# Cross-attention of a decoder layer: half blocks in one order, two projections and two output rows in a run, six places for rotated queries

## The reference

```python
q = (query @ Wq).reshape(nb, q_len, 32, 128).transpose(0, 2, 1, 3)
k = (key @ Wk).reshape(nb, q_len, 8, 128).transpose(0, 2, 1, 3)
v = (value @ Wv).reshape(nb, q_len, 8, 128).transpose(0, 2, 1, 3)
q = q * cos + _rotate_half(q) * sin
k = k * cos + _rotate_half(k) * sin
k, v = jnp.repeat(k, 4, axis=1), jnp.repeat(v, 4, axis=1)
scores = jnp.einsum('bhqd,bhkd->bhqk', q, k) / jnp.sqrt(jnp.float32(128))
scores = jnp.where(mask == 0, jnp.float32(-1000000000.0), scores)
attn = jax.nn.softmax(scores, axis=-1)
x = jnp.einsum('bhqk,bhkd->bhqd', attn, v)
return x.transpose(0, 2, 1, 3).reshape(nb, q_len, 32 * 128) @ Wo
```

## Time and profile before

| | busy us in the span | share |
|---|---|---|
| TensorE matmuls (PE) | 1502.7 | 93% |
| TensorE weight loads (PEld) | 1192.1 | 74% |
| VectorE (DVE) | 1132.3 | 70% |
| ScalarE (ACT) | 458.3 | 29% |
| GpSimd (POOL) | 481.1 | 30% |

### The profile page before, as it was taken

How to read it: one execution, slowest core, us unless ns; L and a number is a source line. 1 busy time by engine, 2 the same in 40 slices (tenths; PEclk the granted TensorE clock), 3 DMA queues, 4 the chain that set the end, 5 groups by cost and what they waited for, 6 DMA issues and landing times. The chain is left out here.

```text
span 1607.8 us, 25367 instructions
## 1 busy us (share of the span) xinstructions
PE 1502.7 (93%) x9824; PEld 1192.1 (74%) x9824; DVE 1132.3 (70%) x1819; ACT 458.3 (29%) x802; POOL 481.1 (30%) x411
## 2 busy tenths in 40 slices
PE   7899978999999569999999999999999999998698
PEld 5688856677777357787778878877877787786476
DVE  3555333688888677787887787787887877886454
ACT  4111133565555221222221221222222212211311
POOL 4322212222222123332432423433333324231022
PEclk9999989999999779999999999999999999999799
DMA  7455211000000221001020110020020201000211
GB/s 231 134 180 171 100 51 39 1 14 21 8 2 1 87 72 52 27 21 60 27 66 14 40 53 27 28 66 22 19 66 27 61 19 40 14 27 1 89 46 59
DMA packets 79107, 83.89 MB, mean 52 GB/s; under 512 B 9824, under 2 KB 50928, under 8 KB 78736
## 3 DMA queue, kind: packets, MB, share of 16 engines
q1 hardware_dynamic: 68976, 63.42, 12.4%
q10 hardware_dynamic: 9216, 16.78, 3.2%
q0 software_dynamic: 800, 2.11, 0.4%
HBM read 59.22 MB, written 23.07 MB: 51 GB/s over the span
## 5 line engine op out<-in xcount | busy, mean ns | idle before, releaser
L1211 POOL TENSOR_TENSOR p_q_rot<-p_ra,p_rb 128x512 f32<-128x512 f32 x128 | 166.9, 1304 | 286.7 <-DVE p_rb L565 286.7
L981 PE MATMUL p_ps_y<-p_wo_hi,p_o_hi 128*128 128x512 f32 x512 | 212.8, 416 | 5.6 <-DVE p_o_lo L1130 5.4
L75 PE MATMUL p_ps_q<-b_xt_hi,p_wq_hi 128*128 128x512 f32 x512 | 211.3, 413 | 0.0
L982 PE MATMUL p_ps_y<-p_wo_lo,p_o_hi 128*128 128x512 f32 x512 | 203.2, 397 | 0.0
L983 PE MATMUL p_ps_y<-p_wo_hi,p_o_lo 128*128 128x512 f32 x512 | 203.0, 396 | 0.0
L76 PE MATMUL p_ps_q<-b_xt_lo,p_wq_hi 128*128 128x512 f32 x512 | 202.4, 395 | 0.0
L77 PE MATMUL p_ps_q<-b_xt_hi,p_wq_lo 128*128 128x512 f32 x512 | 201.2, 393 | 0.0
L1203 POOL TENSOR_TENSOR p_pn<-p_p,p_inv 128x512 f32<-128x512 f32 x64 | 66.8, 1043 | 298.2 <-DVE p_inv L1110 298.2
L1052 ACT ACTIVATE p_o_hi<-p_ps_o 128x512 fp32r<-128x512 f32 x128 | 69.5, 595 | 281.0 <-PE p_ps_o L968 281.0
L1140 DVE TENSOR_TENSOR x_sb<-p_ps_y,x_sb 128x512 f32<-128x512 f32 x128 | 88.0, 688 | 87.3 <-PE p_ps_y L983 87.3
L563 DVE TENSOR_TENSOR p_ra<-p_ps_q,b_cos_t 128x512 f32<-128x512 f32 x128 | 85.9, 671 | 59.8 <-PE p_ps_q L77 56.4
(11 more groups left out here) (179 smaller groups left out, 3163.2 us busy)
## 6 DMA issues: line engine op xcount, KB each, us to landing
p_raw_q<-in_wq SPq DMA_DIRECT2D x36, 256.0 KB, 3.2
v_scratch<-p_v_out SPq DMA_DIRECT2D x32, 256.0 KB, 2.7
k_scratch<-p_k_out SPq DMA_DIRECT2D x32, 256.0 KB, 2.1
p_k_t<-k_scratch ACTq DMA_DIRECT2D x32, 256.0 KB, 2.6
p_v_in<-v_scratch ACTq DMA_DIRECT2D x32, 256.0 KB, 2.8
p_raw_o<-in_wo SPq DMA_DIRECT2D x32, 256.0 KB, 3.6
x_sb<-in_x SPq DMA_DIRECT2D x16, 256.0 KB, 3.1
out<-p_yb SPq DMA_DIRECT2D x16, 256.0 KB, 2.0
```

Of the source, the lines that this page charges most:

```text
L75: nc.tensor.matmul(out, lh, rh, start=(c == 0), stop=False)
L981: nc.tensor.matmul(ps_y[t][:, :], oh, w_hi["o"][h][:, :], start=(h == 0), stop=False)
L982: nc.tensor.matmul(ps_y[t][:, :], oh, w_lo["o"][h][:, :], start=False, stop=False)
L1211: nc.gpsimd.tensor_tensor(q_rot[:, h, :], ra[:, :], rb[:, :], ALU.add).then_inc(q_added, 1)
```

## The change

TensorE's order becomes the same in each half `n`: M(n-1), T(n), S(n+1), two Q, O(n-1, 0), O(n-1, 1), with M(63) and its two O behind the loop. `heads_ahead(n)` names the two Q: in an even half heads 2 and 3 of the next `it`, in an odd half heads 0 and 1 of the one behind it. In front of the loop stand now Q(1,0) and Q(1,1), and only then S(0). `q_rot` has six places instead of four, used in turn (`place`), and the wait of `add_terms` follows that ring.

The raw buffers for q and o are now the same four, so that a load of o waits for the split of q in the same buffer and the other way round. The o weights are waited for head by head in `output`. The low parts of the o weights are made by VectorE for heads 0 and 1 and by GpSimd for heads 2 and 3. The splits for the next group lie in steps 1 (o), 4 and 5 (q) of a group's eight halves. For group 0, ScalarE's exponential of half 0 stands ahead of the four o splits; VectorE does `rotate(1, 0)`, `rotate(1, 1)`, `shift(0)`, two o splits and `invert(0)`; GpSimd does two adds, two o splits and `normalise_p(0)`. The orders of ScalarE, VectorE and GpSimd in the loop follow TensorE's. The buffers keep their total size, and number and sizes of all DMAs and operations are the same.

```diff
-        raw = {"q": [m.sb(f"raw_q{i}", [P, HIDDEN]) for i in range(2)], "o": [m.sb(f"raw_o{i}", [P, HIDDEN]) for i in range(H)]}
+        RING = H + 2
+        raw = [m.sb(f"raw{h}", [P, HIDDEN]) for h in range(H)]
...
-        q_rot = m.sb("q_rot", [P, H, BLOCK])
+        q_rot = m.sb("q_rot", [P, RING, BLOCK])
...
             def load_q(g, h):
-                need(sp, ready["q"], 4 * g + h - 1)
-                sp.dma_start(raw["q"][h % 2][:, :].rearrange("p (c d) -> p c d", c=KC),
-                             wq_dram[:, :, (g * H + h) * D2:(g * H + h + 1) * D2]).then_inc(raw_in["q"][h % 2], 16)
+                need(sp, o_ready[h], g)
+                sp.dma_start(raw[h][:, :].rearrange("p (c d) -> p c d", c=KC),
+                             wq_dram[:, :, (g * H + h) * D2:(g * H + h + 1) * D2]).then_inc(raw_in[h], 16)
 
             def load_o(g, h):
-                need(sp, ready["o"], 4 * (g - 1) + h + 1)
-                sp.dma_start(raw["o"][h][:, :], wo_dram[(g * H + h) * D2:(g * H + h + 1) * D2, :]).then_inc(raw_in["o"][h], 16)
+                need(sp, q_ready, 4 * g + h + 1)
+                sp.dma_start(raw[h][:, :], wo_dram[(g * H + h) * D2:(g * H + h + 1) * D2, :]).then_inc(raw_in[h], 16)
...
-        def split_o_lo(dve, g, h):
+            nc.scalar.activation(w_hi["o"][h][:, :], raw[h][:, :], ACT.Copy).then_inc(part_hi["o"], 1)
+
+        def split_o_lo_vector(dve, g, h):
             need(dve, part_hi["o"], 4 * g + h + 1)
-            nc.vector.tensor_tensor(w_lo["o"][h][:, :], raw["o"][h][:, :], w_hi["o"][h][:, :], ALU.subtract).then_inc(ready["o"], 1)
+            nc.vector.tensor_tensor(w_lo["o"][h][:, :], raw[h][:, :], w_hi["o"][h][:, :], ALU.subtract).then_inc(o_ready[h], 1)
+
+        def split_o_lo_pool(pool, g, h):
+            need(pool, part_hi["o"], 4 * g + h + 1)
+            nc.gpsimd.tensor_tensor(w_lo["o"][h][:, :], raw[h][:, :], w_hi["o"][h][:, :], ALU.subtract).then_inc(o_ready[h], 1)
+
+        def place(it, h):
+
+            return (it * H + h) % RING
+
+        def heads_ahead(n):
+
+            return [(n // 2 + 1, 2), (n // 2 + 1, 3)] if n % 2 == 0 else [(n // 2 + 2, 0), (n // 2 + 2, 1)]
...
-                need(pe, ready["o"], 4 * (n // 2 // NB) + H)
                 need(pe, y_added, n * UT + t - 1)
                 for h in range(H):
+                    need(pe, o_ready[h], n // 2 // NB + 1)
...
+            queries(1, 0)
+            queries(1, 1)
             scores(0)
-            for it in range(ITS):
-                n = 2 * it
-                queries(it + 1, 0)
+            for n in range(HALVES):
+                if n > 0:
+                    mix(n - 1)
+                turn(n)
                 scores(n + 1)
+                for it, h in heads_ahead(n):
+                    queries(it, h)
                 output(n - 1, 0)
-                queries(it + 1, 1)
-                turn(n)
                 output(n - 1, 1)
-                queries(it + 1, 2)
-                mix(n)
-                queries(it + 1, 3)
-                output(n, 0)
-                turn(n + 1)
-                output(n, 1)
-                scores(n + 2)
-                mix(n + 1)
+            mix(HALVES - 1)
             output(HALVES - 1, 0)
...
+            exponentials(0)
             for h in range(H):
                 split_o_hi(act, 0, h)
-            for it in range(ITS):
-                n, g, b = 2 * it, it // NB, it % NB
+            for n in range(HALVES):
+                it, g, step = n // 2, n // (2 * NB), n % (2 * NB)
                 outputs_hi(n - 1)
-                exponentials(n)
-                values_hi(it)
-                if b == NB - 1 and g + 1 < KVH:
+                turned_hi(n)
+                if n % 2 == 0:
+                    values_hi(it)
+                if step == 1 and g > 0:
+                    for h in range(H):
+                        split_o_hi(act, g, h)
+                if step == 4 and g + 1 < KVH:
+                    split_q_hi(act, g + 1, 0)
+                    split_q_hi(act, g + 1, 1)
+                if step == 5 and g + 1 < KVH:
+                    split_q_hi(act, g + 1, 2)
                     split_q_hi(act, g + 1, 3)
                 exponentials(n + 1)
-                turned_hi(n)
-                load_kv(it + 1)
-                if b == 0 and g > 0:
-                    for h in range(H):
-                        split_o_hi(act, g, h)
-                outputs_hi(n)
-                if b == NB - 2 and g + 1 < KVH:
-                    split_q_hi(act, g + 1, 0)
-                    split_q_hi(act, g + 1, 1)
-                turned_hi(n + 1)
-                if b == NB - 2 and g + 1 < KVH:
-                    split_q_hi(act, g + 1, 2)
+                if n % 2 == 0:
+                    load_kv(it + 1)
             outputs_hi(HALVES - 1)
...
             rotate(0, H - 1)
-            for h in range(H):
-                split_o_lo(dve, 0, h)
             dve.wait_ge(masked, 2)
+            rotate(1, 0)
+            rotate(1, 1)
             shift(0)
-            for it in range(ITS):
-                n, g, b = 2 * it, it // NB, it % NB
+            for h in range(2):
+                split_o_lo_vector(dve, 0, h)
+            invert(0)
+            for n in range(HALVES):
+                g, step = n // (2 * NB), n % (2 * NB)
+                add(n - 2, 1)
                 outputs_lo(n - 1)
-                invert(n)
-                rotate(it + 1, 0)
+                turned_lo(n)
                 shift(n + 1)
+                if step == 1 and g > 0:
+                    for h in range(2):
+                        split_o_lo_vector(dve, g, h)
+                first, second = heads_ahead(n)
+                rotate(*first)
+                if n + 1 < HALVES:
+                    invert(n + 1)
+                rotate(*second)
                 add(n - 1, 0)
-                invert(n + 1)
-                rotate(it + 1, 1)
-                turned_lo(n)
-                add(n - 1, 1)
-                if b == 0 and g > 0:
-                    for h in range(H):
-                        split_o_lo(dve, g, h)
-                rotate(it + 1, 2)
-                outputs_lo(n)
-                rotate(it + 1, 3)
-                add(n, 0)
-                turned_lo(n + 1)
-                add(n, 1)
-                shift(n + 2)
+            add(HALVES - 2, 1)
             outputs_lo(HALVES - 1)
...
-                need(pool, s_done, it * 2)
-                nc.gpsimd.tensor_tensor(q_rot[:, h, :], ra[:, :], rb[:, :], ALU.add).then_inc(q_added, 1)
+                need(pool, s_done, 2 * ((it * H + h - RING) // H + 1))
+                nc.gpsimd.tensor_tensor(q_rot[:, place(it, h), :], ra[:, :], rb[:, :], ALU.add).then_inc(q_added, 1)
...
+            add_terms(1, 0)
+            add_terms(1, 1)
+            for h in range(2, H):
+                split_o_lo_pool(pool, 0, h)
+            normalise_p(0)
+            for n in range(HALVES):
+                it, g, step = n // 2, n // (2 * NB), n % (2 * NB)
+                if n % 2 == 0:
+                    values_lo(it)
+                if step == 1 and g > 0:
+                    for h in range(2, H):
+                        split_o_lo_pool(pool, g, h)
+                if step == 4 and g + 1 < KVH:
+                    split_q_lo(pool, g + 1, 0)
+                    split_q_lo(pool, g + 1, 1)
+                if step == 5 and g + 1 < KVH:
+                    split_q_lo(pool, g + 1, 2)
                     split_q_lo(pool, g + 1, 3)
-                normalise_p(n + 1)
-                add_terms(it + 1, 1)
-                add_terms(it + 1, 2)
-                if b == NB - 2 and g + 1 < KVH:
-                    split_q_lo(pool, g + 1, 0)
-                add_terms(it + 1, 3)
-                if b == NB - 2 and g + 1 < KVH:
-                    split_q_lo(pool, g + 1, 1)
-                    split_q_lo(pool, g + 1, 2)
+                first, second = heads_ahead(n)
+                add_terms(*first)
+                if n + 1 < HALVES:
+                    normalise_p(n + 1)
+                add_terms(*second)
```

More of the change, by code:

```diff
@@ L858, in cross_attention @@
         xn_ready, transposed, all_hi, all_lo = (m.sem(n) for n in ("xn_ready", "transposed", "all_hi", "all_lo"))
-        raw_in = {"q": [m.sem(f"raw_in_q{i}") for i in range(2)], "o": [m.sem(f"raw_in_o{i}") for i in range(H)]}
-        part_hi, ready = {w: m.sem(f"part_hi_{w}") for w in "qo"}, {w: m.sem(f"ready_{w}") for w in "qo"}
+        raw_in = [m.sem(f"raw_in{h}") for h in range(H)]
+        part_hi = {w: m.sem(f"part_hi_{w}") for w in "qo"}
+        q_ready, o_ready = m.sem("q_ready"), [m.sem(f"o_ready{h}") for h in range(H)]
         k_in, v_loaded, v_part, v_ready = (m.sem(n) for n in ("k_in", "v_loaded", "v_part", "v_ready"))
@@ L894, in _ @@
                 sp.dma_start(bound[r * SEQ:(r + 1) * SEQ, :, :].bitcast(I32), mask_dram).then_inc(mask_in, 16)
-            for h in range(H):
-                load_o(0, h)
-            for g in range(1, KVH):
```

(13 more changed lines are left out.)

15 lines of the change are left out of this document (2 added, 13 removed).

## The result

The changed kernel takes **1615.33 us**, the median of 8 runs (1613.60 to 1616.61), against 1610.00 for the kernel before (8 runs beside it, 1608.77 to 1611.13): 1.0032 times as long, 95% interval 1.0021 to 1.0043. It is 5.3 us slower. The profiled execution took 1615.7 us, its span is 1613.8, 6.0 more than before.

What follows compares the result with a forecast made beforehand. TensorE, busy 99.99 of 100 us, was taken as the bound, only gaps between its blocks savable. Start 640.7, halves 813.6, waits 0.5, end 36.7 gave 1491.5 against 1488.9, +2.6: forecast 1612.5 us, range 1604.2 to 1619.5.

Steps and rivals of the forecast that it cites:

- same: Whole kernel: outcome within 0.2% of no change, 1606.9 to 1613.3 us; given a chance of 0.4.
- The start: Start of cross-attention: TensorE idle 11.6 us before the first turn, against 5.4 before; loses 8.0 us (6.8 to 9.2).
- The steady state: 59 halves between start and end of cross-attention: 13.79 us each, 0.05 less than before, 813.6 in all.
- I take 0.49, the row with both neighbours: Turn between mix and scores in each half: 0.49 us, read from self-attention's turn behind a mix, ahead of the next scores.
- the 0.5 for waits: Steady halves of cross-attention: 0.5 us allowed for waits at the seven changes of weights.
- rival B: Steady halves: each change of array form paid in full, turn 0.58, 5.3 us more, 1617.8, slower; chance 0.22.
- Self-attention's rows: Self-attention: turn behind a mix takes 0.41 us ahead of a projection, 0.49 ahead of scores; nearest rows for its price.
- the upper end: Turn between mix and scores: 0.58 us, the 0.49 plus the 0.09 that a projection pays ahead of scores.
- The end: Last halves of cross-attention, without queries: 8.8 us each, 36.7 in all against 37.9 before; gains 1.2 us.
- Rival C: A half's chain, likely rotate, add, scores, is longer; 0.2 us beyond the 2 spare costs 12: 1624; chance 0.06.
- Rival A: Row of small blocks: nothing lost, turn 0.35, a half 13.65, 8.3 us less, 1604.2; chance 0.17.
- Rival D: Start of cross-attention differs, for example clock stays full or splits overlap: 3 us less, 1609.5; chance 0.10.

Runs made afterwards that it cites:

- e5_start: Changed kernel, only the order before the loop changed: first scores ahead of the second query, their chain ahead of the second rotate and splits; 1608.45 us, ratio 0.9983.
- e3_mst: Changed kernel with the small blocks in the order mix, scores, turn instead of mix, turn, scores; 1609.07 us (one run).
- e2_tms: Changed kernel with the small blocks in the order turn, mix, scores; 1611.68 us (one run).
- e1_tsm: Changed kernel with the small blocks in the order turn, scores, mix, and VectorE's shift ahead of the outputs' low parts; 1614.61 us, ratio 1.0029.
- e7_mst_start: Changed kernel with the order mix, scores, turn, the shift ahead of the turned block's low part, and the start of e5_start; 1597.20 us, ratio 0.9913.
- e10_mst_start2: e7_mst_start with the first o weights' splits moved ahead of the first scores' chain on ScalarE, VectorE and GpSimd; 1595.77 us, ratio 0.9906.
- e8_double_t: Changed kernel with the four transposes of each turn issued twice over the same data; 1641.64 us (one run).
- e11_before_2t: Kernel before the change with the four transposes of each turn issued twice over the same data; 1637.87 us (one run).

## Why the prediction was right or wrong

**The time** was in the range, 2.8 us above the figure I gave, and slower by 0.3% where I had it within 0.2%. By the last matmul the sum said 2.6 us more, and it was 6.0. I had given "same" and slower 0.4 each.

**The start: right, step by step.** T(0) was forecast at 613.4 after 11.6 idle us and came at 612.24 after 10.99; the whole of cross-attention began 0.7 us earlier than in the profile of before (the rotate of 595.64 stands at 594.92), which is most of that difference. The path was as told: two rotates, shift, exponential, splits on GpSimd, normalise. One reading was 0.2 us off: in the kernel before the clock was full from 604.5 on and not from 604.3 (0.50 in 604.3 to 604.4, 0.68 in the next 0.1 us). It moves no term by more than that. S(1) took 1.98, T(1) and S(2) waited 0.94 and 1.88 where I had 1.2 and 2.1. The start of n=2 was 640.50 against 640.7; since everything had begun 0.7 earlier, the stretch itself took 0.5 more than I had, and the close hit is in part luck. Removing this order (e5_start) gave 7.7 of the 7.8 back.

**The steady state: one term mis-sized.** The failed step is T between M and S, "I take 0.49, the row with both neighbours". It is 0.58. That is 59 x 0.09 = 5.3 us; against it stand the 0.5 for waits, which was not needed (there is no wait), and 0.02 a half from rounding in the other terms (13.86 against 13.88 with T at 0.58). That these lay on the other side was luck: with T's 5.3 alone the time would have been the 1617.8 of rival B. Rival B had the size: T = 0.58, from 0.50 on slower. Of its mechanism the runs bear out half, that T pays for S behind it; "each change of array form is paid in full" fails between M and S (e3_mst, 0.90 and 1.09). I gave it 0.22.

Why I went wrong there can be said. I read T's price from start to start, 0.35, and called the 0.09 behind it a gap, as if it were the same as the 0.09 ahead of S. The two doubled kernels show that it isn't: T costs 0.45 wherever it stands, and the 0.09 behind it is the rest of its own work. So T between full-array blocks never had anything to save. With the prices M 0.91, S 1.08, T 0.45, two Q 5.46 and two O 5.62, a half is 13.52 without any loss. Only T was doubled; M and S are read from start to start, so the borders next to them are known as differences between orders, not as prices. What is above 13.52:

| order of a half | borders between full array and tiled work | half | above 13.52 |
|---|---|---|---|
| before (Q S O Q T O Q M Q O T O S M for two) | 3 | 13.84 | 0.32 (0.04 of it in the Qs, 2.75 instead of 2.73) |
| M T S Q Q O O (the change) | 4 | 13.86 | 0.34 |
| T S M Q Q O O | 2 | 13.71 | 0.19 |
| T M S Q Q O O | 2 | 13.71 | 0.19 |
| M S Q T Q O O | 2 | 13.77 | 0.25 |
| M S T Q Q O O | 2 | 13.65 | 0.13 |

M (64 rows) and S (64 columns) follow each other for nothing. What costs is to go from work on the whole array into tiled work and back, about 0.1 each way, a little less where T is the full-array side (0.08 ahead of S or M, 0.05 behind S or M). The change brings M and S into one row, but sets T, whole-array work, between them. That makes four such borders a half instead of three, two of them the cheaper ones at T, and nothing is gained. The Trainium skill's page "TensorEngine Tiling (Array Packing)" (Key Properties) says that a change of tiling mode drains the engine. The trace agrees in direction where one of the two is the whole array, and gives the size; between M and S, which are two different modes, it shows no loss. The other page of the Trainium skill that I weighed, "TensorE: Matmul & The Clock Gate" (What happens when you issue a matmul), would have had the weights ahead and T at its plain price; with M on one side and S on the other the trace shows 0.58. What exactly is lost at such a border, the drain or a weight load that can't go ahead, no run here separates: the number and the neighbours of the borders are shown as the cause, not what the array does there.

**Self-attention's rows misled a little.** T behind a mix and ahead of whole-array work took 0.41 and 0.49; the 0.41 is what M S T shows too (T behind tiled work, 0.32 behind it). The right sum would have been the 0.49 and the border of 0.09 into S on top, or the 0.41, the 0.09 of its own that shows behind it, and the same border. Either is about 0.58; I had named it as the upper end, and taken the 0.49 without the border.

**The end: right.** 36.41 against 36.5; the three halves without queries are 8.8 long, as worked out.

**Rival C** (a chain that is too long) didn't come in the changed kernel. It did come in e3_mst, where S ahead of T made the low part of an o weight 0.5 late in each group, in e2_tms (0.2), and at the end of e1_tsm. **Rival A** (T 0.35) didn't come: between M and S it is 0.58, next to one of them 0.41 or 0.53, and even where 0.35 shows the price is 0.45. **Rival D**: the start was as I had it.

**The version that beats both** is M S T Q Q O O, with the shift ahead of the turned block's low part, and the first half's own chain ahead of the second rotate and the splits (e7_mst_start, e10_mst_start2): 0.9% shorter than before, with 0.13 us a half above the plain prices instead of 0.32.

## What to carry to other kernels

Group by the form of the array, not by the size of the blocks: a transpose is whole-array work, and put between two tiled blocks it costs as much as what their joining saves. A block's price is read by doubling it, or by the start of the second instruction behind it, never by the start of the first: T was 0.35 by the first and 0.45 by doubling. And when work is moved ahead to fill an idle engine, move the chain of the first item along on every other queue: here 7.8 us hung on the order of a few operations that each run once.

## What the runs showed of the hardware

- A float32 transpose of 128x128 takes 0.11 us in a row of four (0.45), the same between tiled blocks (e8_double_t) and between whole-array blocks (e11_before_2t); there the start of the next block comes 0.10 before that time is over.
- A tiled block of 64 rows and one of 64 columns follow each other without loss (0.91, then 1.08).
- The clock: it fell behind an idle stretch of 3.03 us (S(1) 1.98 in e5_start), and behind 0.94 and 1.88 with 0.7 us of work between them, though there only from 628 on, when S(2) was just done, and in e5_start behind 0.94 and 1.89 while S(2) was running (1.58 instead of 1.15). A single wait of 2.51 had left it at 1.00 in the kernel before; one of 2.02 at the end of the changed kernel was followed by 0.57 (1488 to 1492), the same one of 2.01 in e5_start by 1.00 (1479 to 1486). What decides between these I can't say.
- A gain in a steady state can be paid back in the drain behind it: the profiled execution of e1_tsm won 9 us in 59 halves and lost them behind M(60).
